# A four-layer conditional residual kernel: W1 loaded by column blocks, the ids spread by one matmul, and the set-up lists in another order

## The reference

```python
# layer 0: adapter id e in 0..3 for each sequence, rank 16
x = x + x @ W_base.T + scaling[e] * ((x @ Wt.T @ A[e].T) @ B_w[e].T) @ Wp.T
# layer 1: adapter id f (drawn from 0..6, 8 adapters), rank 16
x = x + x @ W.T + scalings[f] * (x @ A1[f].T) @ Bm[f].T
# layer 2: id g, 8 matrices of 64x64 over the token axis
x = x + einsum('bct,bcd->bdt', x, w2[g])
# layer 3: id h, drawn from 1..198, 200 matrices of 64x64 over the token axis
x = x + einsum('bct,bcd->bdt', x, w3[h])
```

## Time and profile before

| | us |
|---|---|
| median of 3 runs | 172.2 (171.82 to 172.25) |
| the profiled execution | 172.37 |
| its span | 170.2 |
| TensorE busy with matmuls, of the span | 163.6 (96%) |
| VectorE busy | 91.1 (54%) |
| ScalarE busy | 48.5 (28%) |
| GpSimd busy | 86.7 (51%) |
| granted TensorE clock, mean | 0.997 |

### The profile page before, as it was taken

One profiled execution on the slowest core, in us unless ns is written; L12 is line 12 of the kernel. 1 busy time (PEld: TensorE's weight loads), 2 busy tenths in 40 slices (PEclk: granted clock), 3 DMA queues, 4 the chain that ended last, 5 costly groups with the idle time before them and its releaser, 6 DMA issues.

```text
span 170.2 us, 6468 instructions
## 1 busy us (share of the span) xinstructions
PE 163.6 (96%) x2348; PEld 125.0 (73%) x2348; DVE 91.1 (54%) x212; ACT 48.5 (28%) x96; POOL 86.7 (51%) x194
## 2 busy tenths in 40 slices
PE   5889999999999999999999999999999999999992
PEld 5669467678786878687868886877778687868761
DVE  4195975899770846263636645563666180617010
ACT  3142426244230602240223024220503060214021
POOL 4410477764675648475737674756454053608200
PEclk9999999999999999999999999999999999999998
DMA  4799942119550594077309531953394059006406
GB/s 141 252 329 321 282 177 85 33 60 331 190 192 27 168 322 145 23 208 293 131 15 294 209 137 70 285 178 116 123 311 161 31 155 337 2 0 250 123 9 242
DMA packets 16614, 28.75 MB, mean 169 GB/s; under 512 B 3862, under 2 KB 3990, under 8 KB 16598
## 3 DMA queue, kind: packets, MB, share of 16 engines
q1 hardware_dynamic: 14294, 23.31, 41.8%
q0 software_dynamic: 2304, 5.25, 9.1%
HBM read 18.85 MB, written 9.70 MB: 168 GB/s over the span
## 4 chain that ended last, share of the span: by engine, by line
PE 91%; DMA 3%; DVE 1%; SPq 1%; issue 1%; ACT 1%; POOL 0%; DVEq 0%
PE o_ps L751 65%; PE y_ps L751 12%; PE z_ps L751 8%; DMA wb_sb<-in_L_cond_W_base_dram 3%; PE p_ps L751 3%; PE y_ps L764 1%; SPq L231 1%; PE y_ps L811 1%; DVE g L552 0%; PE p_ps L853 0%; DVE b_by L546 0%; ACT o_sb L486 0%; PE p_ps L824 0%; PE z_ps L811 0%; PE p_ps L811 0%
## 5 line engine op out<-in xcount | busy, mean ns | idle before, releaser
L751 PE MATMUL o_ps<-g,yy 128*128 128x512 f32 x384 | 92.1, 395 | 0.0
L751 PEld LDWEIGHTS o_ps<-g,yy 128*128 128x128 f32 x384 | 70.8, 188 | 16.1 <-issue 0.8
L339 POOL COPY u_sel<-u_tab 128x64 f32 x128 | 32.3, 258 | 41.3 <-PE z_ps L751 31.5
L318 POOL DMA_INDIRECT w_all<-in_L_cond_weights_dram,w_rows x32 | 31.8, 994 | 9.6 <-issue 9.6
L631 DVE COPY y_all<-y_ps 128x512 f32<-128x512 f32 x32 | 20.6, 686 | 15.0 <-PE y_ps L751 14.9
L673 DVE COPY o_sb<-o_ps 128x512 f32<-128x512 f32 x15 | 9.7, 687 | 34.5 <-PE o_ps L751 34.5
L426 ACT ACTIVATE yy<-y_all 128x512 fp32r<-128x512 f32 x32 | 19.7, 632 | 16.5 <-DVE y_all L631 16.1
L638 DVE TENSOR_TENSOR yy<-y_all,yy 128x512 fp32r<-128x512 f32 x32 | 21.2, 701 | 3.0 <-ACT yy L426 2.7
L327 POOL DMA_INDIRECT v_sel<-v_table,v_rows x16 | 17.5, 1094 | 6.2 <-issue 6.2
L445 ACT ACTIVATE o_sb<-o_ps 128x512 f32<-128x512 f32 x16 | 8.7, 595 | 37.9 <-PE o_ps L751 37.9
L751 PE MATMUL y_ps<-p_now,x_raw 64*64 64x64 f32 x1024 | 18.6, 221 | 0.0
(11 more groups left out here) (115 smaller groups left out, 104.5 us busy)
## 6 DMA issues: line engine op xcount, KB each, us to landing
x_raw<-in_x_dram SPq DMA_DIRECT2D x16, 512.0 KB, 4.7
out_dram<-o_sb SPq DMA_DIRECT2D x14, 512.0 KB, 5.4
w_sb<-in_L_cond_W_dram SPq DMA_DIRECT2D x4, 256.0 KB, 3.6
wb_sb<-in_L_cond_W_base_dram SPq DMA_DIRECT2D x4, 256.0 KB, 7.1
wp_sb<-in_L_cond_Wp_dram SPq DMA_DIRECT2D x2, 512.0 KB, 6.3
wt_sb<-in_L_cond_Wt_dram SPq DMA_DIRECT2D x1, 1024.0 KB, 8.9
v_table<-v_tab SPq DMA_DIRECT2D x1, 1024.0 KB, 5.7
out_dram<-o_sb SPq DMA_DIRECT2D x4, 256.0 KB, 2.3
```

The costliest lines, as they stand in the source:

```text
L318: pool.indirect_dma_start(out=w3_all[:, j, :], out_offset=None, in_=w3_flat, in_offset=bass.IndirectOffsetOnAxis(ap=w3_rows[:, j:j + 1], a ...
L339: nc.gpsimd.tensor_copy(u_sel[u][:, :, b, RANK * part:RANK * part + RANK], u_tab[:, :, bass.ds(e, 1), :].rearrange("p k a r -> p k (a r)") ...
L751: return nc.tensor.matmul(dst, lhsT, rhs, start=start, stop=stop)
```

## The change

- **W1 by column blocks.** The four transfers of W1 take 128 columns each of all rows, so a piece of a row is 512 B instead of 2 KB; each block gives one chunk g1_k whole. The transposes of block k now stand ahead of what needs g1_k: block 0, the high parts of step 0, block 1, the rest of step 0, block 2, step 1, block 3.
- **The loads' order.** On SyncE's queue W1 and W_base alternate (w1_0, wb_0, w1_1, wb_1, w1_2, w1_3), then Wp, wb_2, a1, a0, w2, scaling and b0, Wt, wb_3, scalings and b1, x.
- **The ids.** Three broadcasts over 128 partitions and three rows leave SyncE's queue. Four rows of 64 ids go to one partition by ScalarE's queue ahead of its first work; VectorE turns them to `fp32r`; one matmul with K = 1 (a row of ones) spreads them over 128 partitions in PSUM, and VectorE copies them to `ids`. `keep_warm` has 11 transposes instead of 16.
- **GpSimd.** It adds the identities in the order of landing, and its gathers start ahead of wb_2 and wb_3: three gathers, wb_2, two, wb_3, six.
- **VectorE.** The work on w3's rows stands between two reads of g1, `scale(E0)` after wpT, the low part of wb_2 ahead of a0T. `place_w2(1)` goes up to right behind `place_w2(0)`, ahead of `v0T` and `scale(E1)`. `add_w3(1)` and the rows of V go ahead of v0g1. The first two copies of y and a low part come ahead of the four reads of v_tab, which run 3, 2, 1, 0; then the low parts of G01.
- **TensorE's tail of the set-up.** `mix(0)` and the first half of step 3 go ahead of v_0 to v_3. These now wait for the copies of y (`yf_set`, 2), mix(1) of turn 0 for v_1, and the token product of quad 1 for v_0. v0g1 uses another bank. The store of `v_table` waits for v_0, the last read, as it did for v_3.

```diff
-            for c in range(KC):
-                sp.dma_start(w1_sb[:, c, :], w1_rows[:, c, :]).then_inc(w1_in[c], 16)
-            for k in range(2):
-                load_wb(k)
-            sp.dma_start(ids[:, 2, :], e3_ids.partition_broadcast(PART)).then_inc(e3_in, 16)
-            for n, t in enumerate((e0_ids, e1_ids, e2_ids)):
-                sp.dma_start(code_ids[:, n, :], t.partition_broadcast(1)).then_inc(code_in, 16)
+            for k in range(KC):
+                sp.dma_start(w1_sb[:, k, :, :], w1_rows[:, k, :, :]).then_inc(w1_in[k], 16)
+                if k < 2:
+                    load_wb(k)
...
+            for n, t in enumerate((e0_ids, e1_ids, e2_ids, e3_ids)):
+                act.dma_start(ids_row[:, n, :], t.partition_broadcast(1)).then_inc(ids_in, 16)
...
+            flip_w1(0)
+            pe.wait_ge(ids_f_set, 2)
+            mm(z_ps[:, 0:4 * BATCH], ones_row[:, :], ids_f[:, :, :].rearrange("p n b -> p (n b)"),
+               True, True).then_inc(ids_spread, 1)
+            g01_high()
+            flip_w1(1)
+            g01_step(0)
+            flip_w1(2)
             g01_step(1)
+            pe.wait_ge(ids_set, 1)
+            flip_w1(3)
...
             place_w2(0)
+            place_w2(1, w2_next)
...
-            place_w2(1, w2_next)
+            add_w3(1, w3_next)
+            find_v_rows()
             dve.wait_ge(setup_act, ACT_DONE["v0g1"])
             read("v0g1", v0g1[0:R0, :], bank_of("v0g1")[0:R0, :], v0g1_low[:, :], ALU.add)
-            add_w3(1, w3_next)
-            find_v_rows()
+            for u in range(2):
+                copy_y(0, u)
+            low_y(0, 0)
             dve.wait_ge(setup_act, ACT_DONE["v0g1_both"])
-            for g in (2, 1, 0, 3):
+            for g in (3, 2, 1, 0):
                 read(f"v_{g}", v_tab[:, g, :], bank_of(f"v_{g}"), v0g1[:, :], ALU.add)
...
             g01_step(2)
-
-            pe.wait_ge(p_set, 1)
+            pe.wait_ge(setup_act, ACT_DONE["gu1"])
+            mix_ready(0, 0)
+            mix(0)
+            g01_step(3, range(0, 2))
+
+            pe.wait_ge(yf_set, 2)
```

More of the change, by code:

```diff
@@ L64, in build @@
         owner = sb("owner", [PART, E1])
-        ids = sb("ids", [PART, 3, BATCH], I32)
-        code_ids = sb("code_ids", [1, 3, BATCH], I32)
+        ids = sb("ids", [PART, 4, BATCH], I32)
+        ids_row = sb("ids_row", [1, 4, BATCH], I32)
+        ids_f = sb("ids_f", [1, 4, BATCH], F32R)
+        ones_row = sb("ones_row", [1, PART], F32R)
+        one = sb("one", [1, PART])
         code_part = sb("code_part", [1, 3, BATCH], I32)
@@ L84, in build @@
         first = ExitStack()
-        w1_sb = sb("w1_sb", [PART, KC, D], of=first)
+        w1_sb = sb("w1_sb", [PART, KC, KC, PART], of=first)
         wp_sb = sb("wp_sb", [PART, KC, D], of=first)
@@ L405, in _ @@
                 read_g1(k)
-            for s in range(0, KC, 2):
-                read(f"wpT_{s}", wpT[:, s, :], bank_of(f"wpT_{s}"))
+            read("wpT_0", wpT[:, 0, :], bank_of("wpT_0"))
+            read("wpT_2", wpT[:, 2, :], bank_of("wpT_2"))
+            high_wb(2)
             read("a1T", a1T[:, 0, :, :].rearrange("p k r -> p (k r)"), bank_of("a1T"))
-            for k in range(2, KC):
-                high_wb(k)
+            high_wb(3)
             read("vu", vu[:, :], bank_of("vu"))
@@ L465, in read_g01 @@
                 read(f"g01_{k}", g01[:, 0, k, :], bank_of(f"g01_{k}"))
+            high_y(0, 0)
             for k in range(2):
                 read_g01(k)
-            high_y(0, 0)
-            read_g01(2)
             high_y(0, 1)
-            read_g01(3)
+            for k in range(2, KC):
+                read_g01(k)
             turn(0, first=True)
@@ L505, in find_w3_rows @@
                     last = nc.vector.scalar_tensor_tensor(
-                        out=w3_rows[half, :], in0=ids[half, 2, :].rearrange("p (j b) -> p b j", b=2)[:, b],
+                        out=w3_rows[half, :], in0=ids[half, 3, :].rearrange("p (j b) -> p b j", b=2)[:, b],
                         scalar=float(SEQ), in1=lane64[half, :], op0=ALU.mult, op1=ALU.add)
@@ L581, in _ @@
             low_wb(0)
-            for k in range(2):
-                low_g1(k)
-            low_wb(1)
-            for k in range(2, KC):
-                low_g1(k)
-            find_w3_rows()
-            scale(E0, b0_in, b0_sb, b0_now, s0_sb)
-            dve.wait_ge(code_in, 48)
-            link(nc.vector.scalar_tensor_tensor(out=code_part[:, 0, :], in0=code_ids[:, 1, :], scalar=float(E0),
-                                                in1=code_ids[:, 0, :], op0=ALU.mult, op1=ALU.add))
+            low_g1(0)
+            dve.wait_ge(ids_spread, 1)
+            nc.vector.tensor_copy(ids[:, :, :].rearrange("p n b -> p (n b)"), z_ps[:, 0:4 * BATCH]).then_inc(ids_set, 1)
+            dve.wait_ge(ids_set, 1)
+            find_w3_rows()
+            low_g1(1)
+            low_wb(1)
+            low_g1(2)
+            link(nc.vector.scalar_tensor_tensor(out=code_part[:, 0, :], in0=ids_row[:, 1, :], scalar=float(E0),
+                                                in1=ids_row[:, 0, :], op0=ALU.mult, op1=ALU.add))
             ef = code_part[:, 0, :].rearrange("p (j b) -> p b j", b=2)
@@ L607, in _ @@
             last.then_inc(code_set, 1)
+            low_g1(3)
             def copy(name, dst, src):
@@ L622, in _ @@
                 read("w2T", w2T[SEQ * b:SEQ * b + SEQ, :, :].rearrange("p g (a j) -> p g a j", j=W2J), w2_bank, eye, ALU.add)
-            for k in range(2, KC):
-                low_wb(k)
+            low_wb(3)
             def copy_y(i, u):
@@ L721, in low_g01 @@
                 read_low(f"g01_{t}", g01[:, 1, t, :], bank_of(f"g01_{t}"), g01[:, 0, t, :])
-            for u in range(2):
-                copy_y(0, u)
-            low_g01(0)
-            low_y(0, 0)
-            for k in range(1, KC):
+            for k in range(KC):
                 low_g01(k)
@@ L955, in turn @@
                 reduce(0)
+                if first:
+                    pe.wait_ge(setup_dve, DVE_DONE["v_1"])
                 mix(1)
+                if first:
+                    pe.wait_ge(setup_dve, DVE_DONE["v_0"])
                 if not last:
@@ L1002, in _ @@
                    True, True).then_inc(setup_ps, 1)
-            g01_step(3, range(0, 2))
-            pe.wait_ge(setup_dve, DVE_DONE["v_1"])
-            mix_ready(0, 0)
-            mix(0)
             g01_step(3, range(2, KC))
```

80 lines of the change are left out of this document (44 added, 36 removed), and 2 rows, old and new, of the table ORDER.

## The result

The changed kernel takes 178.64 us (median of 6 runs, 176.48 to 179.38) against 172.22 us of the kernel before (6 runs): a ratio of 1.035, with a 95% interval of 1.029 to 1.040. The sign is as forecast, the size is not: 6.4 us were lost where 3.0 were forecast, and the time lies above the range. The profiled execution is the shortest of the six, 176.48 us with a span of 174.4; the others took about 2 us more, and a profile of such an execution comes with e1. Every ratio here compares the fast executions of the two kernels alone, those within 1.5% of the kernel's fastest, so it can be smaller than the quotient of the two medians.

A forecast was written before the change was run, and what follows sets the result against it. TensorE, busy 96% of the span, bounds the kernel, with time to win only in the first 25.80 us. +2.6 (`b_by`) and +0.4 (set-up tail) give +3.0 on 172.37: 175.4, median 175.2; range 173.0 to 177.0.

The forecast's parts named there:

- The place and the sign: TensorE's transposes of `b_by` wait for VectorE, making the kernel slower; chance of slower 0.85.
- wb_3's add: GpSimd's add for W_base's last block, forecast near 19.2 us, 0.3 us earlier than before.
- the front of the set-up: TensorE's start up to Wp's transposes: a gain of about 1.8 us, Wp at 13.1 instead of 14.88.
- Five warm-up transposes less: Part of the front on TensorE: fewer warm-ups were to save 1.1 us.
- VectorE's own list: Bound from below if wb_3 came very early: VectorE's work lets `b_by` start at 27.0, still 1.2 us late.
- The term of +2.6: `place_w2(1)` ahead of `v0T` and `b_by` on VectorE makes TensorE's transposes of `b_by` 2.6 us later.
- 28.4: Forecast start, in us, of TensorE's transposes of `b_by`, with wb_3 at 19.2.
- rival 3: Small DMA pieces are dear: W1's blocks up to 2.8 us later, 177.0, possibly with a clock fall; chance 0.10.
- x of quad 1: Its load waits behind the later store of `v_table`, so TensorE waits 0.35 us; bounds 0 and 1 us.
- Wt and `vu`: Middle of the set-up: Wt lands near 18.4, so `vu` starts about when it did, taking back the front's gain.
- W1's pieces of 512 B: W1's DMA in 2048 smaller pieces delays wb_3 by 0.7 us.
- The other half: Broadcasts and rows of ids gone from the DMA queue: worth 1.0 us to wb_3.

The follow-up runs named there:

- e1: The changed kernel run again, unaltered: 177.8 us against 172.25 for the kernel before, ratio 1.031.
- e2: The changed kernel with only `place_w2(1)` put back behind the work on cross: 174.07 us against 172.25 for the kernel before, ratio 1.010.
- e6: The kernel before with only `place_w2(1)` moved up behind `place_w2(0)`: 181.16 us against 179.17 for the kernel before, ratio 1.015.
- e7: The kernel before with 11 warm-up transposes instead of 16: 179.21 us against 179.17 for the kernel before, ratio 1.001.
- e5: The changed kernel with `place_w2(1)` back and quad 1's first x load ahead of the `v_table` store: 181.16 us against 179.17 before, ratio 1.013.
- e14: The same kernel as e5, run again: 184.46 us against 179.62 for the kernel before, ratio 1.025.
- e17: The same kernel as e2, run again on another chip: 181.76 us against 179.77 for the kernel before, ratio 1.008.
- e9: The same kernel as e6, run again: 182.97 us against 180.04 for the kernel before, ratio 1.015.
- e18: The same kernel as e6, run again: 183.38 us against 179.77 for the kernel before, ratio 1.015.
- e3: The changed kernel with 16 warm-up transposes instead of 11: 177.66 us against 172.25 for the kernel before, ratio 1.022.
- e4: The changed kernel with `place_w2(1)` back and 16 warm-up transposes: 173.7 us against 172.25 for the kernel before, ratio 1.009.
- e11: The same kernel as e8, run again: 181.32 us against 180.04 for the kernel before, ratio 1.000.
- e8: e5's kernel with 16 warm-ups and three more transposes filling pauses around the ids matmul: 181.03 us against 179.17 for the kernel before, ratio 1.013.

## Why the prediction was right and wrong

- **The place and the sign** held. "A wait of TensorE for `b_by` of 2 to 3.5 us, by far its longest" is 2.4 us; wb_3's add was forecast near 19.2 and came at 19.27; the time from the transposes of `b_by` to turn 0, forecast as the same, is 42.05 - 29.46 = 12.6 us as before. e1 against e2 shows that the move makes the wait: 2.4 us with it, 0.2 without, and nothing else changed; e6 against e7 shows the same place 2.9 us later in the kernel before.
- **The step that failed first: "the front of the set-up (gain, about 1.8 us up to Wp)".** Wp's transposes came at 15.40, not 13.1: 0.5 us lost where 1.8 were to be won. The step took the matmuls of steps 0 and 1 to run as in the kernel before, at 0.24 us; ten or so ran at 0.41, since the clock rose at 11.25 us instead of 5.42. Where it rose early, with the same 11 warm-ups, Wp came at 13.1 to 13.5 (e5, e14, e17), near the forecast: the error is to have taken a pace for a constant of the instruction. "Five warm-up transposes less save 5 x 3.67/16 = 1.1 us" is too much as well: nothing in the kernel before (e7), about 0.4 us at Wp in the changed one.
- **Which bound decides.** The forecast let wb_3 gate `b_by` and took VectorE's own list as the lower bound, 27.0 us for Wp at 13.1. With Wp at 15.40 that bound moves 2.3 later, to 29.3, and `b_by` came at 29.46. The profile shows it: w2T ended at 21.65 and wb_3's low part followed at 21.68 without a wait, though wb_3's high part was there at 20.38. The term of +2.6 is +3.66 measured in this execution, 1.1 more, and by this reading from the error in the front; no profile has `place_w2(1)` ahead and a fast start together, so that 28.4 would have come then is not shown.
- **The term that was missing: the clock behind the wait.** It stood only as a rider of rival 3 ("it could come with a fall of the clock"), at 0.10 together with dear pieces. It was missing from the sum, and it is the larger part of what the common execution lost beyond the first profile: e1 lost 1.5 us by it, e6, e9 and e18 ran v0g1 in 3.78 us instead of 2.12, and of the changed kernel's twelve runs where before takes 172.2 eleven have a mean clock of 0.99 or less. It belonged in the forecast: the new wait of 3 us was its own result.
- **x of quad 1**, forecast at 0.35 us between 0 and 1: 0.25 in the first profile, 0.8 in e1, 1.0 in e2, and 1.4 in e3, over the upper bound. Mechanism right, shown by the seven profiles without it; the size was taken too small for most executions.
- **Wt and `vu`.** Wt landed 9.6 us behind its issue at 9.01, at 18.6 (forecast 18.4). `vu` started at 19.96 all the same, because VectorE was late with a0T: wb_2's low part and b0's scaling now stand ahead of it. This wait of 0.8 us was not seen; it costs nothing here, since the wait for `b_by` comes after it, but where that wait is gone, all of `vu`'s lateness counts (e2, 1.38 us). In the fast starts it is Wt for which TensorE stands, 0.8 to 2.1 us (e4, e5, e11, e14, e17).
- **W1's pieces of 512 B.** The change's profile has a stretch of almost nothing but these, from 6.0 to 6.5 us:

```profile
DMA packets 320, 0.16 MB, mean 325 GB/s; under 512 B 3, under 2 KB 320, under 8 KB 320
```

  That is 325 GB/s against 389 for pieces of 2 KB, 25 ns a piece where the straight line gave 30. For 1 MB it is 3.2 us instead of 2.7: +0.5 where the sum had +0.7. The last of the first six blocks was at GpSimd at 9.51 us instead of 8.31. The rule of the Trainium skill (DMA: Bandwidth & Descriptors, Specifications), 512 B as the least size at line rate, is near but not exact here: these pieces ran 16% under the larger ones. The other half held: without the broadcasts the DMA share from 7 to 9 us was 1.12 and 1.05 instead of 0.52 and 0.41, and wb_3 came 0.24 us earlier (forecast 0.3).

So the sum against this execution: +3.66 at `b_by` (forecast 2.6), 0.25 for x (0.4), 0.2 spread behind it: +4.1. The common execution has 2.2 us more, mostly the clock; e1's sum is 29.82 - 25.80 = 4.0 at `b_by`, 1.5 for the clock and 0.8 for x, 6.3 of the 178.75 - 172.37 = 6.4 us by which it is longer.

What stays open: why the clock rises late in some executions of the change and in none profiled of before's kind; how often it does in executions without a profile; why the same wait of 2.4 us is followed by a fall of the clock in e1 and not in the first profile; and what the load of x ahead of the store is worth.

## What to carry to other kernels

When a step is moved ahead on an engine, look first for who waits for the instruction that it passes: here 2.9 us of copies that cost nothing behind `cross` cost 3.7 to 5.7 us ahead of `b_by`, because VectorE and TensorE met there within 0.2 us. Waits of 1.5 to 3.2 us on TensorE had a second price behind them in most profiles here (e1, e3, e4, e5, e6, e17), the work that then ran at the lower clock; put it into the sum, with a chance, whenever the sum itself yields such a wait. And a chain that has no slack is forecast by the later of its gates, each recomputed with what the rest of the change does to it, not by the one that held before.

## What the runs showed of the hardware

- A mean clock of 1.00 over the first microseconds does not exclude half pace. In the first profile the window from 5 to 12 us reads 1.00, while 8 matmuls 128x512 took 0.41 us each, and 12 took 0.25 each from 12.13 on. The trace's first record of the clock opens at 11.25 us, and what lies ahead of it counts as 1.00; the pace of equal matmuls shows it, and so does the start of that record. In the kernel before it opens at 5.42, and there 16 warm-up transposes took 0.23 us each.

```profile
5.00:12.00 7.00, 6.82 (x22) 5.05 (x21) 4.36 (x11) 1.72 (x3) 3.67 (x6) 1.00 1.05 359
```

- The same wait of 2.4 us for `b_by` was followed by a fall of the clock in e1 (0.58 over 4.1 us) and by none in the first profile (1.00). Shorter waits were followed by a fall too: 1.5 us in e4, 1.7 in e17 and 2.1 in e5, each time to 0.50 or 0.51 from 19.4 to 22.8 us; none came behind 1.4 us in e11 and 0.8 in e14.
- Chips differ by 4%: the kernel before took 172.2 us on one and 179.2 to 180.0 on four others, and the profiles of the other kernels on those four have pauses of up to some microseconds between 24 and 37 us that no semaphore explains. The ratio of one kernel moved with them, from 1.031 to 1.040 for the change and from 1.000 to 1.013 for one and the same experiment (e11, e8).
